# Attention and a quantised feed-forward on one core: maxima sent in two halves, and a new order of a head pair's products on TensorE

## The reference

```
xn  = layernorm(x)                                    # 8 batches, 1024 rows, 512 columns
qkv = xn @ W_attn + b_attn                            # 16 heads of 32 columns
att = softmax(where(causal, q @ k.T * 32**-0.5, -inf))
y   = (att @ v) @ W_proj + b_proj
q4(t): per block of 16: scale = max|t| / 6, round t/scale to {0,.5,1,1.5,2,3,4,6}, times scale
ffn = q4(silu(q4(xn) @ q4(w_gate).T) * (q4(xn) @ q4(w_up).T)) @ q4(w_down).T     # 1408 hidden
out = x + y + ffn
```

## Time and profile before

| | us |
|---|---|
| median of 3 runs | 3561.23 (3561.09, 3561.23, 3565.2) |
| profiled execution, its own time | 3565.72 |
| its span in the trace | 3563.9 |
| PE busy | 3499.0 (98%) |
| PEld (weight loads) busy | 2677.9 (75%) |
| DVE busy | 2672.9 (75%) |
| ACT busy | 1214.2 (34%) |
| POOL busy | 1071.6 (30%) |
| granted TensorE clock, mean | 0.995 |

### The profile page before, as it was taken

One profiled execution on the slowest core, in us unless ns is written; L12 is line 12 of the kernel. 1 busy time (PEld: TensorE's weight loads), 2 busy tenths in 40 slices (PEclk: granted clock), 3 DMA queues, 4 the chain that ended last, 5 costly groups with the idle time before them and its releaser, 6 DMA issues.

```text
span 3563.9 us, 55622 instructions
## 1 busy us (share of the span) xinstructions
PE 3499.0 (98%) x20212; PEld 2677.9 (75%) x20212; DVE 2672.9 (75%) x4872; ACT 1214.2 (34%) x2164; POOL 1071.6 (30%) x512
## 2 busy tenths in 40 slices
PE   7999999999999999999999999999999999999999
PEld 6667667677576676676765688888888888888887
DVE  6776867877777768678777677777777777777776
ACT  2542533634625425336345222222222222222222
POOL 1770952834817709528347100000000000000000
PEclk9999999999999999999999999999999999999999
DMA  6535446346365364463465411010011011011010
GB/s 216 140 99 189 105 140 179 83 154 173 84 201 136 103 190 103 142 177 83 156 192 174 146 35 32 30 35 32 29 35 32 29 35 32 29 35 32 29 35 30
DMA packets 182897, 348.96 MB, mean 98 GB/s; under 512 B 42961, under 2 KB 50641, under 8 KB 181841
## 3 DMA queue, kind: packets, MB, share of 16 engines
q1 hardware_dynamic: 158256, 291.75, 28.5%
q10 hardware_dynamic: 24480, 55.06, 4.3%
HBM read 225.19 MB, written 120.00 MB: 97 GB/s over the span
## 4 chain that ended last, share of the span: by engine, by line
PE 88%; DVE 5%; DMA 3%; issue 2%; ACT 1%; SPq 1%; POOL 1%; ACTq 0%; POOLq 0%; DVEq 0%
PE f_ps L1702 27%; PE ps_dense L1176 14%; PE f_ps_o L1714 13%; PE ps_st L1228 8%; PE ps_s L1201 5%; PE ps_y L1254 4%; PE ps_dense L1254 3%; PE ps_dense L1342 3%; PE ps_dense L1201 2%; PE f_ps L1694 2%; PE ps_st L1240 1%; PE ps_dense L1266 1%; PE ps_s L1342 1%; DMA stack<-mr 1%; DMA arena<-mr 1%
## 5 line engine op out<-in xcount | busy, mean ns | idle before, releaser
L1702 PE MATMUL f_ps<-wgu,xqt 128*128 128x512 f32 (+1 forms) x4608 | 990.0, 372 | 2.8 <-DVE xqt L1557 1.4
L1702 PEld LDWEIGHTS f_ps<-wgu,xqt 128*128 128x128 f32 x4608 | 840.1, 188 | 123.4 <-DVE h L1576 1.8
L771 DVE CUSTOM_DVE_ANT_0 ps_s<-ps_s,row_mask 128x640 f32<-128x640 f32 (+3 forms) x512 | 529.3, 1034 | 100.9 <-PE ps_s L1201 91.8
L1714 PE MATMUL f_ps_o<-wd,hqt 128*128 128x512 f32 x2112 | 512.5, 395 | 0.6 <-DVE hqt L1583 0.6
L1714 PEld LDWEIGHTS f_ps_o<-wd,hqt 128*128 128x128 f32 x2112 | 392.0, 188 | 79.4 <-DVE hqt L1583 0.8
L1176 PE MATMUL ps_dense<-arena,wa 128*128 128x512 f32 x1536 | 376.4, 394 | 1.2 <-DVE stage L828 1.0
L1077 ACT ACTIVATE pt<-ps_st 128x512 f32<-128x512 f32 (+1 forms) x512 | 273.5, 571 | 239.4 <-PE ps_st L1228 226.2
L696 POOL TENSOR_TENSOR stage<-pt 128x1792 f32<-128x1792 f32 x41 | 165.1, 4028 | 604.2 <-ACT pt L1080 564.1
L1080 ACT ACTIVATE pt<-ps_st 128x512 f32<-128x512 f32 (+1 forms) x512 | 278.6, 572 | 180.7 <-PE ps_st L1228 76.2
L1176 PEld LDWEIGHTS ps_dense<-arena,wa 128*128 128x128 f32 x1536 | 284.1, 188 | 58.9 <-DVE stage L828 2.4
L698 POOL TENSOR_TENSOR stage<-stage,pt 128x1536 f32<-128x1536 f32 (+2 forms) x107 | 322.0, 3009 | 9.4
(11 more groups left out here) (164 smaller groups left out, 5468.6 us busy)
## 6 DMA issues: line engine op xcount, KB each, us to landing
qk_scratch<-stage SPq DMA_DIRECT2D x128, 512.0 KB, 3.0
stack<-qk_scratch SPq DMA_DIRECT2D x192, 256.0 KB
arena<-qk_scratch SPq DMA_DIRECT2D x192, 256.0 KB
xs<-in_L_attn_x SPq DMA_DIRECT2D x64, 256.0 KB, 3.7
acc_scratch<-rob ACTq DMA_DIRECT2D x64, 256.0 KB, 2.0
xt<-in_L_attn_x SPq DMA_DIRECT2D x64, 256.0 KB, 2.6
at<-acc_scratch SPq DMA_DIRECT2D x64, 256.0 KB, 2.6
out<-ot SPq DMA_DIRECT2D x64, 256.0 KB, 2.0
```

The source lines that it names most:

```text
L771: nc.vector.tensor_tensor_reduce(row, row, row_mask[:, S - keys:S], -1.0, LARGEST, ALU.add, ALU.min, mx[:, h * ST + q:h * ST + q + 1]).the ...
L1702: last = nc.tensor.matmul(ps[:, SLOT[c], gu, 0:n].rearrange("p (j n) -> p j n", n=P), xqt[:, a, k], wgu[:, b, gu * FC + f // P:gu * FC + ( ...
L1714: last = nc.tensor.matmul(ps_o[:, :], hqt[:, a, k], wd[:, b, k], start=i == 0, stop=i == len(terms) - 1)
```

## The change

Four edits.

1. **Maxima.** SyncE sends the high half after `m_hi` and the low half after `m_lo`, where both waited for `m_lo`.
2. **Order of a pair** (`STEPS`). `P4` and `P5` go from the next pair's first key tile to the end of their own pair. `P3` goes from u = 7 to u = 5, in the place of `P2`, and `P2` goes to the start of the next pair, ahead of `S0`. The first `T` of a pair is issued ahead of `S0` too. In u = 2 the mask `M2` is issued after `DEN P0` rather than ahead of them. In u = 7 `M0` follows its `S0` at once.
3. **Dense stage** (`BESIDE`). The transpose and the split of pair 0's maxima go from the second third of QK13 to the first third of QK14.
4. **Second unit's store.** The store of the last unit of a batch, issued by ScalarE, is moved from the batch's end to behind QK1 of the next batch.

```diff
-    STEPS = ["S0 T S1 P4 P5 T T S2 S3 M3",
+    STEPS = ["T P2 S0 T S1 T S2 S3 M3",
              "S0 T P6 P7 S1 T S2 S3 M3",
-             "T S0 S1 T S2 M2 DEN P0 T T",
+             "T S0 S1 T S2 DEN P0 M2 T T",
              "S0 S1 T S2 M2",
              "S0 S1 T T M1",
-             "P1 P2 MAX T S0 S1 M1",
+             "P1 P3 MAX T S0 S1 M1",
              "S0 T M0",
-             "S0 T P3 M0 T"]
+             "S0 M0 T P4 P5 T"]
...
-    BESIDE["QK", 13, 1] = "MAX"
+    BESIDE["QK", 14, 0] = "MAX"
...
             def maxima(p):
 
-                sp.wait_ge(m_lo, ONE + b * PAIRS + p + 1)
-                for j in range(2):
+                for j, part in enumerate((m_hi, m_lo)):
+                    sp.wait_ge(part, ONE + b * PAIRS + p + 1)
                     sp.dma_start(stack(p)[KS + j:KS + j + 1, 0:2]...
...
+                if i == 1 and b:
+                    store_unit(b - 1, rest_of(b - 1), beside_projection(False)[1])
...
             high_of_unit(two)
-            store_unit(two)
+            if final:
+                store_unit(b, rest, two)
```

More of the change, by code:

```diff
@@ L454, in batches_in_line, with rest_of @@
             body(b, b == B - 1)
+    def rest_of(b):
+        for first, end, matrix, unit in REST:
+            if first <= b < end:
+                return matrix, unit - first
     def batches_and_rest_in_line(body):
@@ L1008, in high_of_unit, with store_unit @@
                 nc.scalar.activation(unit_space[i % 2][:, 3].bitcast(F32R), ps_y[:, :], ACT.Copy).then_inc(q_hi, 1)
-            def store_unit(i):
+            def store_unit(b, rest, i):
                 matrix, u = unit_of(b, rest, i)
@@ L1114, in body @@
                 if k == 6:
-                    store_unit(one)
+                    store_unit(b, rest, one)
             high_of_unit(two)
-            store_unit(two)
+            if final:
+                store_unit(b, rest, two)
         batches_and_rest_in_line(body)
```

## The result

| | before | changed |
|---|---|---|
| median of the runs, us | 3561.16 (3552.79 to 3565.2, 4 runs) | 3532.95 (3530.77 to 3535.09, 4 runs) |
| ratio | | 0.9924, 95% interval 0.9905 to 0.9943 |
| profiled execution, us | 3565.72 | 3533.86 |
| its span | 3563.9 | 3532.1 |

The change takes 28 us off the median, and 31.9 between the two profiled executions. The forecast was 3533.

A forecast was written before the change was run, and what follows sets the result against it. It took TensorE's own work (88% of the chain) and its waits for the maxima's landing as the bound. Terms 12.1 + 9.5 + 12.9 + 0.5 - 2.4 = 32.6 off 3565.7 gave 3533 us, range 3525 to 3550.

The forecast's parts named there:

- the clock term: Behind pair 7: cold stretches go, winning 5.6 us each in batches 1 and 5, 1.7 in the last; gain 12.9.
- The landing bounds each step, and there is no reserve: At each pair's first score S0: the maxima's DMA landing releases it, so any delay of the landing counts in full.
- Pair 7, 9.5: At its first S0: cover and earlier landing of 1.31 us; even batches lose their 1.06 wait; gain 4.2 + 5.2.
- no stretch below 1.00: Sign expected in the changed profile: TensorE's clock shows no cold stretch before the feed-forward's end.
- The first rival: At pair 7 of odd batches: waits over 1 us still lower the clock, giving back up to 12.9, 3546 us; chance 14%.
- the argument on pair 7's other work: Behind pair 7: cold stretches priced from measured rows, 5.6 us, not the rule's 6.8, as not all time is array time.
- Pairs 1 to 6, 12.1: At their first S0: 1.3 us cover plus 0.31 earlier landing remove most waits, 13.4 us, less 1.3; gain 12.1.
- Costs of the order, 1.3 and 2.4: 1.3 not won where pair 1 meets GpSimd's sums of pair 0; 2.4 lost at pair 7, four scores sharing three banks.
- Dense stage, 0.5: The wait at MAX, about 0.5 us a batch, goes; about 0.4 reappears four matmuls on; gain 0.5 over eight batches.
- M2, P2, store: nothing: Later mask, moved P2 and second unit's store: no effect, bounds of 0.1 us a batch either way for each.
- The high half as "0.31 us": First maxima DMA can start at 411.90 instead of 412.21, so each pair's last landing comes 0.31 us earlier.
- Own signs: Expected in the profile: maxima waits fall from 24 to about 4, steady pairs stay 17.5 us, pair 7 waits for ScalarE.

The follow-up runs named there:

- the delayed maxima: One more small SyncE DMA ahead of each pair's two maxima DMAs: kernel before with it 3628.5 us, changed kernel with it 3544.75 us.

## Why the prediction was right, term by term

The forecast of 3533 (3532.95 measured) is right in its mechanism and in most terms. That it is exact is luck. It subtracted 32.6 from a profiled execution that lies 4.5 above the median, and the medians are only 28.2 apart. Between the profiles, where 31.9 were won, the clock term was 5.0 too large, and some 3.3 us that no term stood for made up most of that.

- **The landing bounds each step, and there is no reserve.** Right, and shown by the delayed maxima (70 us against 12).
- **Pair 7, 9.5.** Right. Waits left in the odd batches were forecast as 1.67, 1.19, 1.50 and 1.12; `MAX` to S0 is now 4.77, 4.38, 4.87 and 4.54, that is 1.44, 1.05, 1.55 and 1.21 behind the earliest possible start, 5.25 in sum for 5.48. Gain 15.0 - 5.25 = 9.7.
- **Clock, 12.9: the mis-sized term.** "I take this in full" was wrong, and so was "no stretch below 1.00". Batches 1 and 5 still lose 2.6 us each, and 1.6 was won in batch 7. Setting batch 2's pair 7 against the others, the clock gave back 7.9 us: 3.0, 3.3 and 1.6. The first rival (waits over 1 us still bring the clock down) was partly true, and cost 5.0 of the 12.9. The pricing rule that the prediction weighed (the Trainium skill, TensorE: Matmul & The Clock Gate, Terms) gives half the length, so 3.4 us for the stretches of about 7 us that remain. The trace says 2.6, and for the 14 us of before 5.6 and 6.0 against 6.8: the rule overprices both here, as the argument on pair 7's other work had it.
- **Pairs 1 to 6, 12.1.** Right. Their late steps are 15.7 us over 3.45 in sum; what the three in batch 7 lose beyond the new distance of 5.02 is 1.6, so 14.1 were won, where 13.4 was taken. All waits for maxima there are gone.
- **Costs of the order, 1.3 and 2.4.** Nearly right. With the recovered waits taken out, a batch takes 0.3 to 0.7 us more in the new order, 4.3 in eight. Pair 7 accounts for 3.0 where 2.4 was taken: it takes 18.36 us for 18.99 though P4 and P5, 1.00 us, left it. The other 1.3 is as taken. Pair 1 is 0.1 to 0.4 us longer, where `DEN` waits for GpSimd in all eight batches (3.7 us in 8 waits) rather than in three, and the pairs behind it give some of that back.
- **Dense stage, 0.5.** 1.1 in the rows, too little for the measured times to tell.
- **M2, P2, store: nothing.** For the store the times agree, though the profiles leave room for a microsecond or two. M2's cover was not the copy of the denominators alone but also DEN's wait; the two nearly cancel. P2 was not tried alone.
- **The high half as "0.31 us".** Right as a difference in the changed kernel, misleading as a price. Alone it wins 20 us. The prediction named the packet of the instruction queue beside the long waits and read it as a delay of fixed size. It is a collision: in batch 1 the landing due at 3.09 us after `MAX` came in time beside a packet that began at 2.82, and the one due at 3.40 beside a packet begun at 2.79 came at 5.32.
- **Own signs.** The wait at `mx` went, four waits on `arena` under 1.5 us stayed, steady pairs held 17.5, ScalarE appeared in pair 7: all as said. The wait four matmuls on in the dense stage came too, 0.2 us, though the view puts it down to issue and not to line 779. The cold stretch at pair 7's S0, named as a sign of a wrong forecast, appeared twice.

Adding up, in us: 14.1 - 1.3 (pairs 1 to 6) + 9.7 - 3.0 (pair 7) + 7.9 (clock) + 1.1 (dense stage) = 28.5 of the 31.9 between the profiles. The remaining 3.3 or so lie ahead of, between and behind the pairs, where no term of the forecast stood.

## What to carry to other kernels

Where a consumer starts just as its data lands in every instance, the profile shows no wait, and yet there is no reserve. Look at the distance from producer to consumer, and delay the transfer on purpose to see what is hidden. Pulling independent products ahead of the consumer is worth more than its visible waits, but see what else those products keep apart: here the same two products also kept a score tile off a bank that was still being reduced. A gain from a small shift of timing may be luck with where other packets fall; shift the program by some instructions, and see what is left. A DMA that is issued late can also stand behind another engine's wait: look at the issue before the transfer is blamed.

## What the runs showed of the hardware

- **Instruction packets of the busiest engine delay small transfers.** TensorE's 16 KB packets, 0.9 to 1.7 us each on a DMA engine, went with landings 0.5 to 1.9 us late of 8 KB transfers that otherwise take 1.8. 64 more instructions at the start moved 14 of 16 such places, and the time by 10 us. The Trainium skill (Runtime: NRT & Kernel Launch, Instruction fetch mechanics) gives blocks of 256 instructions, which agrees with the spacing here, and describes the fetch as mostly hidden; TensorE's matmuls in attention of the kernel before show no idle time put down to issue, so the trace agrees for the engine that fetches, and not for its neighbours' transfers.
- **The length of a wait doesn't decide the clock.** In the kernel with M2 back, pair 7 waits 0.96 us in batch 3 and 0.95 in batch 5:

```profile
948.01 0.97 PE L1236 MATMUL ps_st<-arena 98*128 98x512 f32 x4 [0.96 <-DMA arena<-mr]
1432.43 0.97 PE L1236 MATMUL ps_st<-arena 98*128 98x512 f32 x4 [0.95 <-DMA arena<-mr]
...
950.50:957.30 6.80, 6.80 (x45) 3.77 (x41) 0.70 (x2) 3.75 (x8) 3.72 (x1) 0.50 0.47 189
```

  The first is followed by 6.8 us at 1.2 GHz, the second by none. With the dense edit alone, `MAX` to S0 of 4.88 us in batch 1 was followed by 13.7 us cold, and the longer 5.12 in batch 5 by 3.4. What decides between them, no run here shows.
- **A delay of 0.79 us in 56 steps is 44 us of waiting; it cost 70.** The rest is probably mostly clock: attention has sixteen cold stretches, 88.7 us in all, for three of 30.7 us in all before. At 5.6 us for each 13.7, as in batch 1, the 58 more come to 24 us, which is an estimate.
